# Attention scores of two heads in the two row halves of TensorE: float32r level pairs in place of three bf16 levels

## The reference

```
q, k, v = heads(x @ Wq + bq), heads(x @ Wk + bk), heads(x @ Wv + bv)     # layer 0
scores  = q @ k.T / sqrt(16) + slope[h] * (j - i)                        # ALiBi slopes per head
y       = softmax(where(j <= i, scores, -inf)) @ v

a1 = softmax(causal(q1 @ k1.T / sqrt(16)))                               # layer 1: two maps per head
a2 = softmax(causal(q2 @ k2.T / sqrt(16)))
y  = normalise((a1 - lambda[h] * a2) @ v)
```

## Time and profile before

| what | value |
|---|---|
| median of 3 runs (lowest to highest) | 5924.18 us (5909.79 to 5935.9) |
| span of the profiled execution | 5916.1 us |
| PE matmul busy | 5058.1 us, 85% |
| DVE busy | 3390.4 us, 57% |
| ACT busy | 2567.7 us, 43% |
| POOL busy | 1828.3 us, 31% |

### The profile page before, as it was taken

The page is one execution under the profiler, slowest core; times in us unless marked ns, Lnnn a source line. Parts: engine busy times, 40 slices in busy tenths (PEclk is TensorE's granted clock), DMA queues, the critical chain, the costliest instruction groups (busy, mean ns, idle before and its releaser), DMA issues. The chain is left out here.

```text
span 5916.1 us, 82750 instructions
## 1 busy us (share of the span) xinstructions
PE 5058.1 (85%) x29088; PEld 2711.9 (46%) x29088; DVE 3390.4 (57%) x6345; ACT 2567.7 (43%) x5102; POOL 1828.3 (31%) x1800
## 2 busy tenths in 40 slices
PE   6566489999978566499987999999999999799996
PEld 3455333333325455357973333333333333255896
DVE  7511468887846721241119788878888878343111
ACT  2311217776662311132215176766766766513221
POOL 2388311111101288534331122222222222104332
PEclk9778779999989687699998899999999999889998
DMA  3476561222213277606986411221221221120798
GB/s 107 116 148 149 138 171 33 62 58 68 62 53 104 76 156 151 149 26 212 330 269 198 108 37 40 63 49 40 64 47 40 64 48 40 55 69 1 267 318 268
DMA packets 503528, 659.28 MB, mean 111 GB/s; under 512 B 147310, under 2 KB 358318, under 8 KB 497998
## 3 DMA queue, kind: packets, MB, share of 16 engines
q1 hardware_dynamic: 370158, 500.99, 27.0%
q0 software_dynamic: 133056, 154.15, 13.2%
HBM read 489.33 MB, written 164.20 MB: 110 GB/s over the span
## 5 line engine op out<-in xcount | busy, mean ns | idle before, releaser
L1724 DVE TENSOR_REDUCE ea_mx<-ea_psA 128x1 f32<-128x512 f32 (+3 forms) x2304 | 1373.9, 653 | 242.0 <-PE ea_psA L1585 144.1
L1706 ACT ACTIVATE ea_pr<-ea_psB 128x512 f32<-128x512 f32 (+3 forms) x2560 | 1198.9, 535 | 567.4 <-PE ea_psB L1608 557.7
L1585 PE MATMUL ea_psA<-ex_kx,ex_qx 99*128 99x512 bf16 (+3 forms) x2560 | 868.4, 357 | 20.2 <-DVE ea_mx L1724 13.3
L1608 PE MATMUL ea_psB<-ex_qx,ex_kx 99*128 99x512 bf16 (+3 forms) x2560 | 846.2, 349 | 0.0
L1724 DVE TENSOR_REDUCE ba_mx<-ba_psA 128x1 f32<-128x512 f32 (+3 forms) x1152 | 686.2, 653 | 144.3 <-PE ba_psA L1585 95.6
L1706 ACT ACTIVATE ba_pr<-ba_psB 128x512 f32<-128x512 f32 (+3 forms) x1280 | 601.5, 536 | 288.9 <-PE ba_psB L1611 155.5
L1625 PE MATMUL ea_psO<-ea_pr,ea_vx 128*32 128x512 f32 (+3 forms) x5120 | 603.5, 543 | 20.9 <-POOL ea_pr L1554 14.0
L1585 PEld LDWEIGHTS ea_psA<-ex_kx,ex_qx 99*128 99x128 bf16 x2560 | 250.3, 98 | 551.8 <-DVE ea_mx L1724 427.8
L1585 PE MATMUL ba_psA<-bx_kx,bx_qx 108*128 108x512 bf16 (+3 forms) x1280 | 443.5, 364 | 7.8 <-PEq L1146 4.5
L1608 PE MATMUL ba_psB<-bx_qx,bx_kx 108*128 108x512 bf16 (+3 forms) x1280 | 424.9, 349 | 14.6 <-DMA bx_qx<-ba_mT 14.4
L1608 PEld LDWEIGHTS ea_psB<-ex_qx,ex_kx 99*128 99x128 bf16 x2560 | 246.5, 98 | 310.3 <-ACT ea_pr L1706 141.0
(11 more groups left out here) (528 smaller groups left out, 8260.9 us busy)
## 6 DMA issues: line engine op xcount, KB each, us to landing
de_wg<-in_L_rg SPq DMA_DIRECT2D x64, 512.0 KB, 4.7
de_wu<-in_L_ru SPq DMA_DIRECT2D x64, 512.0 KB, 5.9
de_wd<-in_L_rd SPq DMA_DIRECT2D x64, 512.0 KB, 7.3
fe_wg<-in_L_rg SPq DMA_DIRECT2D x64, 512.0 KB, 4.9
fe_wu<-in_L_ru SPq DMA_DIRECT2D x64, 512.0 KB, 5.9
fe_wd<-in_L_rd SPq DMA_DIRECT2D x64, 512.0 KB, 7.5
ae_w<-in_L_w SPq DMA_DIRECT2D x64, 384.0 KB, 3.6
ce_w<-in_L_w SPq DMA_DIRECT2D x64, 384.0 KB, 3.8
```

The costliest lines, as they stand in the source:

```text
L1585: last = nc.tensor.matmul(psA[:, slot, at:at + n], qx[0:KB, s, hh, t * P:(t + 1) * P], kx[0:KB, s, hh, k:k + n], start=True, stop=not diag)
L1608: last = nc.tensor.matmul(psB[:, slot, off:BLK], kx[0:KB, s, hh, kt * P:(kt + 1) * P], qx[0:KB, s, hh, Q * BLK + off:(Q + 1) * BLK], start ...
L1706: nc.scalar.activation(pr[:, j % 4, hh, off:BLK], psB[:, exp_slot(n), off:BLK], ACT.Exp).then_inc(s_exp, 1)
L1724: v.tensor_reduce(out, src, AX.X, ALU.max).then_inc(s_ar, 1)
```

## The change

Queries and keys are stored as two float32r levels (the second holds what the first leaves over), in float32 tiles. Three pairs of levels (`Q_LEVELS`, `K_LEVELS`) make 48 rows, with the bias rows 50 or 54, so that one head fits in 64 partition rows. `qx` and `kx` are now `[128, 2, 2, 2048]`: heads 0 and 2 lie in rows 0 to 63, heads 1 and 3 in rows 64 to 127. PE's list holds `B` and `A` in pairs, so that neighbours read different halves:

```diff
-LEVEL_PAIRS = ((0, 0), (0, 1), (0, 2), (1, 0), (1, 1), (2, 0))
-KP = len(LEVEL_PAIRS) * DH
+Q_LEVELS, K_LEVELS = (0, 0, 1), (0, 1, 0)
+KP = len(Q_LEVELS) * DH
+HALF = P // 2
...
-        lev = sc.sb("lev", [P, NL, 3, BLK], BF16)
+        lev = sc.sb("lev", [P, NL, 2, BLK], F32R)
...
-                    nc.vector.tensor_tensor(res[:, u, :], t32[:, u, :], lev[:, v, 0], ALU.subtract).then_inc(s_c, 1)
-                    dve.wait_ge(s_c, base + n * 2 + 1)
-                    nc.vector.tensor_copy(lev[:, v, 1], res[:, u, :]).then_inc(s_c, 1)
-                    dve.wait_ge(s_c, base + n * 2 + 2)
-                    nc.vector.tensor_tensor(lev[:, v, 2], res[:, u, :], lev[:, v, 1], ALU.subtract).then_inc(s_lo, 1)
+                    nc.vector.tensor_tensor(lev[:, v, 1], t32[:, u, :], lev[:, v, 0].bitcast(F32),
+                                            ALU.subtract).then_inc(s_lo, 1)
...
-            out += [(t, k0, m, (h, h + 1)) for h in (0, 2)] if m <= BLK // 2 else [(t, k0, m, (h,)) for h in range(HV)]
+            out += [(t, k0, m, (h, h + 2)) for h in (0, 1)] if m <= BLK // 2 else [(t, k0, m, (h,)) for h in range(HV)]
...
-        for i in items:
+        for i in items[::2]:
             while done * weights > passed * total and where < len(slots) - 1:
                 where += 1
-                passed += _WEIGHT[slots[where]]
-            put(slots[where], "A", (d, i))
-            done += COST[i]
+                passed += weight(slots[where])
+            for own in (i, i + 1):
+                put(slots[where], "A", (d, own))
+                done += COST[own]
...
-        if hh == 2 and (j >= 2 or with_prev):
+        if hh == 1 and (j >= 2 or with_prev):
             order.append(("V", j - 2))
...
-                        last = nc.tensor.matmul(psA[:, slot, at:at + n], qx[0:KB, s, hh, t * P:(t + 1) * P],
-                                                kx[0:KB, s, hh, k:k + n], start=True, stop=not diag)
+                        r0 = hh % 2 * HALF
+                        last = nc.tensor.matmul(psA[:, slot, at:at + n], qx[r0:r0 + KB, s, hh // 2, t * P:(t + 1) * P],
+                                                kx[r0:r0 + KB, s, hh // 2, k:k + n], start=True, stop=not diag)
                         if diag:
-                            last = nc.tensor.matmul(psA[:, slot, at + n - P:at + n], C["identb"], C["maskA"],
-                                                    start=False, stop=True)
+                            for x in range(2):
+                                last = nc.tensor.matmul(psA[:, slot, at + n - P:at + n], C[f"identb{x}"][r0:r0 + HALF],
+                                                        C[f"maskA{x}"][r0:r0 + HALF], start=False, stop=x == 1)
...
-                    c.link(v.scalar_tensor_tensor(r, m, -1.0, lv[:, :, 0, :], ALU.mult, ALU.subtract))
-                    c.link(v.tensor_copy(lv[:, :, 1, :], r))
-                    v.tensor_tensor(lv[:, :, 2, :], r, lv[:, :, 1, :], ALU.subtract).then_inc(s_L, 1)
+                    v.scalar_tensor_tensor(lv[:, :, 1, :], m, -1.0, top, ALU.mult, ALU.subtract).then_inc(s_L, 1)
...
+            for n, dst in kept.items():
+                sp.dma_start(dst.rearrange("r j s -> r (j s)"), D[n].rearrange("r j s -> r (j s)")).then_inc(s_kept, 16)
...
-    lv = [scratch(f"lv{i}", (3, B * H, S), BF16) for i in range(4)]
+    lv = [scratch(f"lv{i}", (2, B * H, S)) for i in range(4)]
+    kept = {n: scratch(f"kept_{n}", D[n].shape) for n in ("c_q", "c_k", "c_q1", "c_k1")}
```

More of the change, by code:

```diff
@@ L14 @@
 BF16 = mybir.dt.bfloat16
+F32R = mybir.dt.float32r
 I32 = mybir.dt.int32
@@ L1287 @@
 _OWN = sum(_WEIGHT[:NEXT_AT]) / sum(_WEIGHT)
-CUT = next(i for i in range(NA) if sum(COST[:i]) >= (1 - _OWN) * sum(COST))
+CUT = next(i for i in range(0, NA, 2) if sum(COST[:i]) >= (1 - _OWN) * sum(COST))
 M_LATER, K_AT, C_AT = 6, 10, 23
@@ L1368, in load_keys @@
[L1368 to L1378 removed]
+        self.of_step = of_step
@@ new lines, in __init__, with keys_in, keys_after, constant @@
+        self.NQ = 2 * len(Q_LEVELS) + 2
+    def keys_in(self, st):
+        return 2 * len(K_LEVELS) + (2 if st < 2 or self.of_step else 0)
+    def keys_after(self, st):
+        return sum(self.keys_in(n) for n in range(2 - st % 2, st + 1, 2))
+    def constant(self, a, st, half):
+        return a[ds((st * 2 + half) * self.F, self.F)] if self.of_step else a
+def level_rows(lv, level, st, half):
+    if len(lv) == 2:
+        return lv[half][level, ds(st * (2 * DH), 2 * DH), :].rearrange("(j d) s -> d j s", d=DH)
+    return lv[0][level, ds(st * (HV * DH), HV * DH), :].rearrange("(j q d) s -> q d j s", q=2, d=DH)[half]
@@ L1391, in attention_phase @@
         mx = sc.sb("mx", [P, QB, HV, KT])
[L1392 to L1394 removed]
+        m8 = sc.sb("m8", [P, HV, 8])
+        ml = [sc.sb(f"ml{k}", [P, HV * 2 * tc], F32R) for k, (_, tc) in enumerate(KINDS)]
+        mT = sc.sb("mT", [P, len(KINDS), P])
         osb, rec = (sc.sb(n, [P, 2, S]) for n in ("osb", "rec"))
@@ L1607, in scores @@
                     slot = exp_slot(n)
-                    last = nc.tensor.matmul(psB[:, slot, off:BLK], kx[0:KB, s, hh, kt * P:(kt + 1) * P],
-                                            qx[0:KB, s, hh, Q * BLK + off:(Q + 1) * BLK], start=True, stop=two or r < 0)
-                    if r >= 0 and not two:
-                        last = nc.tensor.matmul(psB[:, slot, off:off + P], C["identb"], C["maskB"],
-                                                start=False, stop=True)
+                    r0, diag = hh % 2 * HALF, r >= 0 and not two
+                    last = nc.tensor.matmul(psB[:, slot, off:BLK], kx[r0:r0 + KB, s, hh // 2, kt * P:(kt + 1) * P],
+                                            qx[r0:r0 + KB, s, hh // 2, Q * BLK + off:(Q + 1) * BLK],
+                                            start=True, stop=not diag)
+                    if diag:
+                        for x in range(2):
+                            last = nc.tensor.matmul(psB[:, slot, off:off + P], C[f"identb{x}"][r0:r0 + HALF],
+                                                    C[f"maskB{x}"][r0:r0 + HALF], start=False, stop=x == 1)
                     last.then_inc(s_b, 1)
@@ L1762, in _ @@
                 v.memset(mx[:], NEG_BIG).then_inc(s_none, 1)
-                for k in range(1, NK):
-                    v.memset(ml[k][:], 0.0)
                 dve.wait_ge(s_none, 1)
@@ L1982, in bf16, with two_levels @@
     return np.asarray(a, np.float32).astype(mybir.dt.np(BF16))
-def three_levels(a):
-    a, out = np.asarray(a, np.float32), []
-    for _ in range(3):
-        out.append(bf16(a))
-        a = a - out[-1].astype(np.float32)
-    return out
-BIAS_ROWS, BIAS_MAX = 12, 3
+def two_levels(a):
+    a = np.asarray(a, np.float32)
+    top = (a.view(np.uint32) & np.uint32(0xFFFFF000)).view(np.float32)
+    return top, a - top
+BIAS_ROWS = 6
 F32_CONSTS = (("ident", P), ("code", NT), ("dummy", 1), ("ecol1", E0), ("lower", NG0 * NG0), ("rev1", E1),
```

142 lines of the change are left out of this document (67 added, 75 removed).

## The result

The changed kernel takes 6162.9 us (median of 4 runs, 6138.12 to 6187.72) against 5923.93 of the kernel before (4 runs): 1.041 times as long, 95% interval 1.0388 to 1.0434. The profiled execution spans 6166.8 us, 250.7 more than before. It lies outside the forecast's range, and the kernel became slower where it was to become faster.

What follows compares the result with a forecast made beforehand. PE was taken to bound full units, DVE 15% behind. Steps gain 80 us, less 5 for projections and 10 for the start: 65 off the span, 5916.1 to 5851, median 5860 us; range 5740 to 6090, own range 5800 to 5900.

Steps and rivals of the forecast that it cites:

- The products: Float32r products of `A` and `B`: one pass each, at bf16's 0.215 us per 512 columns.
- the halves: Two matmuls in different row halves: full overlap taken, a pair costing 0.215 us; with none, 0.43.
- the masks: One more mask matmul per masked `A`, in `ba` also `B`: 3.7 us of PE each, half counted, 1.8 a step.
- 1.26 worked out: DVE's level chain: two linked instructions less, three times, 1.26 us of DVE a step, 0.7 counted as gain.
- The loads: Query and key loads and the maxima's DMAs queued behind: no net effect, 0 us, bounds -40 to +15.
- A full unit after: Full units: DVE becomes the bound, waiting 0.18 us; 2.83 falls to 2.58 us, 6.0 us a step over 24 units.
- The clock, my rival at 8%: PE, held by DVE, falls to 1.2 GHz; a third of the time there loses 139 us: 6080 us, chance 8%.
- the signs that would prove me wrong: Pairs starting 0.2 us apart, a clock at 0.5 within steps, or PE waiting for the maxima's DMAs every step.
- a third of the time: Lower clock, units of 3.8 us: a third there gives 2.99, worse than 2.83; a fifth eats the gain.
- My argument against it: Experts hold clock 1.00 with PE busy 7.10 of 10 us; PE would still issue some 2 of 2.6 us.
- The start: Kernel start: 3.15 MB of constants copied ahead of the gate weights PE awaits, -10 us, bounds 0 and -14.
- The projections: Stores of `lv` grow by a third: `ep` has room, `bp` costs between nothing and 18 us; -5 counted.

Runs made afterwards that it cites:

- even_fill: v_between with POOL's multiplication and `C` later, pairs of `A` spread evenly over units, and unit 1's `B`s made twice; 5867.4 us, 0.9908 of the kernel before.
- v_between: Changed kernel with `V` placed between the two pairs of `A` and the four `B`s behind them; 5958.8 us, 1.0071 of the kernel before.
- busy_half: Changed kernel with the products of B2 and B3 made twice in full units, to fill PE's pause; 6130.8 us, 1.0347 of the kernel before.
- late_fill: v_between with POOL's multiplication moved to unit 24, `C` behind it, and all `B`s of unit 1 made twice; 5879.1 us, 0.9939 of the kernel before.
- same_half: Changed kernel with the four `B`s in head order 0, 2, 1, 3, so neighbours share a row half; 6313.9 us, 1.0667 of the kernel before.
- no_overlap: v_between with POOL's multiplication and `C` later, and heads 0, 2, 1, 3 in `A` and `B`; 6020.5 us, 1.0150 of the kernel before.

## Why the prediction was wrong

**The products, the halves and the masks were right.** The runs show one instruction per product, pairs that overlap, 0.23 us from pair to pair in a flow (0.215 assumed). DVE is 1.35 us a step less busy in `ea` (1.26 worked out). The masks cost about half of their time, as counted. The loads cost nothing: the waits for the maxima in `ba`, 16.9 us before, are gone, though in longer steps; even_fill, with shorter ones, has one of 6.5 us.

**The step that failed is "A full unit after".** Its mechanism was right, DVE as the bound with a gap because three banks do not cover `V`, but the round was 2.26 us, not 1.95 (1.98 with the late weight load). By the rows: 0.07 from the freed bank (3906.03 + 0.68 = 3906.71) to the late `A`; 0.66 from there to `V`, for which I had 0.43 and part of `V`'s two changes; 0.99 of `V`; and 0.54 until DVE reads, where I had bf16's 0.42. The first product after a pause is 0.11 us longer than one in a flow, 0.50 for 0.39, and the late `A` splits the pairs. DVE's gap is 0.45 for 0.18, the unit 2.93 for 2.58, and the gain of 6.0 us a step became a loss of 2.4 in 24 units. v_between is the proof by repair: `V` moved by two products, the gap 0.23, a step of 106.3, and 105.0 without the collision, where I had forecast 104.5 for the order that the change really has.

**The clock, my rival at 8%, came on top of it.** It costs more than the waits: about 130 of 210 us in `ea` by the estimate above. Of the signs that would prove me wrong, a clock at 0.5 within steps is the one that came. Its price was somewhat low: 3.8 us for a unit of 2.58 is 0.32 us lost for each at the lower level, and 0.37 and 0.39 were measured in the changed kernel. The prediction took a third of the time for a third of the units there: 2.99 us is the mean when a third of the units are slow; a third of the time would make 2.89, and over a quarter of the time, not a fifth, would have eaten the gain. A little over a fifth of `ea` lay there (0.89); but there was no gain to eat. My argument against it, PE busy 7.10 of 10 us in the experts at 1.00, did not carry over. busy_half and late_fill show that filling PE's pauses keeps the clock higher. The Trainium skill, "TensorE: Matmul & The Clock Gate", section "A second HAM failure mode: psum-queue depth-cycling", describes short idle times between groups of matmuls that make the clock swing; the pauses of 0.3 to 0.8 us here agree.

**Smaller terms.** The start cost 3.7 us for my 10. PE's first matmul, in the changed kernel and then in the kernel before:

```profile
26.99 3.30 PE L277 MATMUL an_psT<-all_cf,an_xn 128*128 128x128 f32 x16 [26.99 <-DMA an_gate<-in_L_gate]
```
```profile
23.27 3.65 PE L276 MATMUL an_psT<-all_cf,an_xn 128*128 128x128 f32 x16 [23.27 <-DVE an_xn L225]
```

The projections cost 23 us for my 5: `bp` 13.3, inside its bounds, but `ep`, which I gave room, 9.8. DMA is busy 0.81 of `ep`'s time for 0.69, and its clock is 0.96 for 1.00. Which of the two holds `ep` was not tried.

**What stays open.** What makes the clock fall is only in part shown: same_half and no_overlap both put neighbours into one half; the first had more time at the lower clock, the second less. Pauses explain the falls that late_fill and busy_half took away, but not this pair.

## What to carry over

When a change makes one engine faster, write out the round that the next one waits in (bank freed, product, what stands in between, product, read) with recorded lengths from start to read, and count how many banks it must span; place the long instruction where the ring is fullest. A faster PE that then pauses can lose its clock, as here, so price the pauses at both levels, and look at the granted clock before looking at busy time. And when an order moves, see which long instruction on a neighbour engine it now meets.

## What the runs showed of the hardware

A DVE instruction of 0.18 us, from SBUF to SBUF, lasted 4.41 us beside a POOL multiplication of 4.51, and seven such cost 29 us; in the kernel before one instruction of the chain had met the multiplication too (4.50 us). The Trainium skill, "SBUF — State Buffer", section "Who interferes with whom", says that a DVE instruction in a two-port mode and a GpSimd instruction shut each other out for their whole length; the rows agree in that DVE's instruction lasts as long as the multiplication, but in which mode it ran none of them shows.

Products that nobody reads made the kernel faster: 64 in `ea` and 32 in `ba` took some 34 us off (5913 to 5879).
